# One buffer for the residual, deeper scratch, ScalarE in the preparation, and new orders for every engine

## The chip, the cores and the metric

The kernel runs on one core of one Trainium2 chip. A core has TensorE (PE), VectorE (DVE), ScalarE (ACT), GpSimd (POOL) and SyncE (SP), which here issues all DMAs. The metric is the device time of one launch in microseconds, from the inputs in memory to `out_y` in memory.

## What is computed

The reference is two transformer layers on x of shape (16, 256, 256), in float32. Each sublayer is added to its input and layer-normalised.

```python
x = L0_attn_x                                   # (16, 256, 256), heads of 16
x = _layernorm(x + _L0_attn_ref(x, ...))        # stage a
x = _layernorm(x + _L0_ffn_ref(x, ...))         # stage g, first half
x = _layernorm(x + _L1_attn_ref(x, ...))        # stages g (qkv), b, e
x = _layernorm(x + _L1_ffn_ref(x, ...))         # stage c
# _L0_attn: q, kv = x @ W.T; both through an fft over 16, l2-normalised per head;
#           kv summed over the sequence (cumsum); product; ifft; @ W_o.T
# _L0_ffn : 8 experts; gate = sigmoid(slope * (sum((w_n . (x - m_n)/|x - m_n|)**2) - center));
#           the best expert's low-rank update (rank 8) and bias, mixed with x by the gate
# _L1_attn: softmax attention, 16 heads of 16, on a qkv reshaped without a transpose
# _L1_ffn : ternary weights (groups of 64): W -> sign-like {-1,0,1} * mean|W|;
#           h = relu(x @ w1.T)**2; rmsnorm(h) @ w2.T, hidden 1024
```

The order of the batches is free, since each of the 16 is computed alone.

## The kernel before, in words

Everything of a batch is two sides of 128 partitions with 256 columns. A batch goes through stages whose names begin with a letter: `a` (first attention), `g` (gated feed-forward, and then q, k and v of the second attention), `b` (the maxima of the scores, the pass before the softmax), `e` (scores, exponentials, output), `c` (ternary feed-forward). `w` is the preparation of weights, which is done once, `p` the load of x.

Each engine runs a list of steps of its own. A step is a short Python function of the same name that waits for semaphores and issues a few instructions. `turns` (L605) walks three lists one after the other for each engine: FILL, written out as `step@batch`, up to turn 8; then ORDER, in which `step:+shift` means the batch that is that many turns behind (with the stage's lag in LAG, L97), repeated for turns 8 to 13; then DRAIN, written out again. Within an engine nothing passes anything else: a step that waits holds all that is behind it in its list. So the lists and the semaphores together set the time, and several batches are under way at once (in the middle, stage `c` works on the batch five behind the one in stage `a`).

The preparation starts with five loads on SP, all counted by one semaphore, `dft_in`: constants, the two DFT matrices and three weights. PE multiplies weights by the DFT matrices into pA and pC. DVE splits each product into a rounded high part (`fp32r`) and the difference (L1295, L1296), copies the inverse one (L1298), splits the qkv weights in the same way (`w_qkv_split`, L1332, L1333), and makes the ternary weights: `w_scale` casts 2,048 columns to bf16 (L1257) and reduces them, four `w_sign` steps compare and multiply them, PE turns them (`w_turn`) and ACT copies them out. Every one of these DVE instructions waits for the one before it (`prep`).

A batch's second residual lives in three places. `g_res2` and `g_norm2` write it into `x2`; `b_keep` on ACT copies `x2` into `xb[k]`, one of two; `e_res` adds the attention's output and writes `x3[k]`, one of two, from which stage `c` reads until `c_res`. `g_res2` of the next batch waits for the copy of this one.

For the second attention q and k are split into three bf16 parts (high, middle, low), written to scratch in memory (`g_out_0`, `g_out_1`, `g_out_2`) and read back in another layout (`g_in_0` with six DMAs, `g_in_1` with four, `g_in_2` with two). The scratch is two deep for q and k and one deep for v. `b_max_0`, PE's first score product of the max pass, waits for all twelve. PE then alternates between two banks, which DVE's maxima (`b_max_read`, L1545) free; the row maxima go back into qT by way of `b_rows`. `g_gate1` and `g_gate2` on DVE are the gate's small steps, with `g_exp` on ACT between them.

Of the kernel before, what the change touches and what calls it, by code (L numbers as in the profile page):

```python
# [107 lines left out]

# [7 lines left out]

# [1684 lines left out]
```

## Time and profile before

| | us |
|---|---|
| median of three runs (lowest, highest) | 824.48 (819.50, 828.29) |
| the profiled execution | 822.42 |
| its span, first to last instruction | 820.4 |

| engine | busy us | share |
|---|---|---|
| PE | 679.6 | 83% |
| DVE | 595.2 | 73% |
| ACT | 477.4 | 58% |
| POOL | 354.0 | 43% |

The mean granted clock of TensorE is 0.931 of full speed. The profile's page cuts the span into 40 slices of 20.5 us and gives each engine's busy tenths in each. Tables by stage give the same sums in microseconds for a chosen stretch. A timeline row is one instruction, or several alike that follow one another, with the idle time before it in square brackets and what ended it.

### The profile page before, as it was taken

The numbers are of one execution on the slowest core, as the hardware profiler recorded it, in microseconds if no ns is written. First come the engines' busy times: TensorE is split into PE (matmuls) and PEld (weight loads), VectorE is DVE, ScalarE is ACT, GpSimd is POOL, SyncE is SP. The second block draws the span as 40 slices with busy tenths as digits, with TensorE's granted clock in tenths as the row PEclk, the third lists the DMA queues.
The fourth block names the chain that finished last, engine by engine and source line by source line (L and its number), as shares of the span: only waits on it lengthen the run. The fifth ranks groups of instructions, "written<-read, shape, count | busy, mean of one in ns | idle before, by whom it ended". The sixth has DMA issues, their size and how long they took to land.

```text
span 820.4 us, 14805 instructions
## 1 busy us (share of the span) xinstructions
PE 679.6 (83%) x5100; PEld 530.1 (65%) x5100; DVE 595.2 (73%) x1429; ACT 477.4 (58%) x961; POOL 354.0 (43%) x537
## 2 busy tenths in 40 slices
PE   3545667788999999999999999899997998888773
PEld 3324545465777778787777777777776776656462
DVE  3977548687888797979797879688888877457120
ACT  0123232646767677777676767677657485755930
POOL 3214202112536464645454645352647253354554
PEclk9667688999999999999999999999999999999976
DMA  6100044716071617171617162506162525350000
GB/s 210 51 0 14 14 71 104 131 19 136 13 140 37 120 41 138 34 138 32 135 37 133 39 136 49 119 26 111 33 111 71 96 61 85 83 118 28 14 13 14
DMA packets 298170, 60.57 MB, mean 74 GB/s; under 512 B 237352, under 2 KB 293616, under 8 KB 298096
## 3 DMA queue, kind: packets, MB, share of 16 engines
q1 hardware_dynamic: 298096, 59.63, 36.0%
q8 instruction: 41, 0.67, 0.3%
q14 instruction: 33, 0.27, 0.1%
HBM read 38.38 MB, written 20.97 MB: 72 GB/s over the span
## 4 chain that ended last, share of the span: by engine, by line
PE 41%; DVE 20%; SPq 14%; DMA 9%; ACT 6%; issue 5%; POOL 5%; POOLq 0%; DVEq 0%; ACTq 0%
SPq L710 9%; PE pA L892 7%; DVE nmax L1545 6%; PE pB L908 5%; PE pA L807 4%; PE pO L960 4%; DMA kT<-qk_scratch 4%; DMA qk_scratch<-qk_part 3%; PE pC L1009 3%; PE pC L1031 3%; SPq L696 2%; PE pS L934 2%; PE pS L984 2%; PE pA L791 2%; DMA xa<-in_x 1%
## 5 line engine op out<-in xcount | busy, mean ns | idle before, releaser
L1545 DVE TENSOR_REDUCE nmax<-pB 128x2 f32<-128x512 f32 x256 | 167.5, 682 | 49.5 <-PE pB L908 48.7
L1160 ACT ACTIVATE pt<-pS 128x512 f32<-128x512 f32 x256 | 149.4, 605 | 84.6 <-PE pS L934 83.3
L908 PE MATMUL pB<-kT,qT 96*128 96x256 bf16 x512 | 93.5, 284 | 30.0 <-DMA kT<-qk_scratch 15.7
L1720 POOL TENSOR_TENSOR hsum<-hsum,hsq 128x512 f32<-128x512 f32 x48 | 63.0, 1312 | 86.3 <-ACT hsq L1200 86.3
L934 PE MATMUL pS<-qT,kT 98*128 98x256 bf16 x512 | 88.5, 277 | 6.8 <-ACT pt L1160 5.4
L1743 POOL TENSOR_TENSOR hid_lo<-hh,hid 128x512 fp32r<-128x512 f32 x64 | 86.1, 1345 | 2.9 <-ACT hh L1210 2.6
L908 PEld LDWEIGHTS pB<-kT,qT 96*128 96x128 bf16 x512 | 40.0, 100 | 60.7 <-DVE nmax L1545 32.7
L1009 PE MATMUL pC<-x3T,w1T 128*128 128x256 f32 x256 | 71.2, 311 | 4.3 <-ACT hr L1188 2.6
L960 PE MATMUL pO<-pt,v_ext 128*32 128x256 f32 x1024 | 71.0, 397 | 3.7 <-ACT pt L1160 3.6
L1009 PE MATMUL pC<-x3T_lo,w1T 128*128 128x256 f32 x256 | 65.4, 289 | 0.0
L934 PEld LDWEIGHTS pS<-qT,kT 98*128 98x128 bf16 x512 | 42.4, 98 | 34.7 <-ACT pt L1160 16.1
L1031 PE MATMUL pC<-w2T,hid 128*128 128x256 f32 x256 | 63.7, 290 | 0.8 <-DVE ms L1605 0.8
L892 PE MATMUL pA<-xgT,w_qkv 128*128 128x256 f32 x192 | 60.5, 315 | 2.8 <-ACT qkv L1123 1.9
L1031 PE MATMUL pC<-w2T,hid_lo 128*128 128x256 f32 x256 | 61.9, 283 | 0.0
L892 PE MATMUL pA<-xgT,w_qkv_lo 128*128 128x256 f32 x192 | 55.7, 290 | 0.0
L892 PE MATMUL pA<-xgT_lo,w_qkv 128*128 128x256 f32 x192 | 55.7, 290 | 0.0
L1009 PEld LDWEIGHTS pC<-x3T,w1T 128*128 128x128 f32 x256 | 50.5, 197 | 6.8 <-ACT hr L1188 3.9
L1665 POOL TENSOR_SCALAR vea<-mva 128x2 f32<-128x2 f32 x16 | 5.4, 337 | 112.6 <-DVE mva L1346 112.6
L1009 PEld LDWEIGHTS pC<-x3T_lo,w1T 128*128 128x128 f32 x256 | 50.8, 198 | 0.0
L1031 PEld LDWEIGHTS pC<-w2T,hid 128*128 128x128 f32 x256 | 49.1, 192 | 1.5 <-DVE ms L1605 1.0
L1123 ACT COPY qkv<-pA 128x512 f32<-128x512 f32 x48 | 29.9, 622 | 34.7 <-PE pA L892 34.6
L1031 PEld LDWEIGHTS pC<-w2T,hid_lo 128*128 128x128 f32 x256 | 49.2, 192 | 0.1
(175 smaller groups left out, 1750.2 us busy)
## 6 DMA issues: line engine op xcount, KB each, us to landing
qk_scratch<-qk_part SPq DMA_DIRECT2D x48, 256.0 KB, 5.1
...
xa<-in_x SPq DMA_DIRECT2D x16, 256.0 KB, 3.8
v_scratch<-qkv SPq DMA_DIRECT2D x16, 256.0 KB, 3.4
v_heads<-v_scratch SPq DMA_DIRECT2D x16, 256.0 KB, 3.1
out_y<-y SPq DMA_DIRECT2D x16, 256.0 KB, 3.0
...
```

The source lines that it names most:

```text
L710: sp.dma_start(dst[r:STACK:PARTS, :].rearrange("d (h n) -> d h n", h=HEADS), scratch[k, n].rearrange("(w h d n) -> w d h n", w=2, h=HEADS, ...
L807: ins = pe.matmul(dst, part, w, start=(first and n == 0), stop=(last and n == 2))
L892: ins = pe.matmul(pA[1][:, half * T:(half + 1) * T], w[:, c, cols], part[:, c, :], start=(c == 0 and q == 0), stop=(c == CH - 1 and q == 2))
L908: ins = pe.matmul(pB[h % 2][:, s * T:(s + 1) * T], qT[k][0:STACK, u * P:(u + 1) * P], kT[k][0:STACK, h * T:(h + 1) * T], start=True, stop= ...
L934: ins = pe.matmul(pS[h % 2][:, s * T:(s + 1) * T], kT[k][:, u * P:(u + 1) * P], qT[k][:, h * T:(h + 1) * T], start=True, stop=True)
L960: ins = pe.matmul(pO[32 * j:32 * (j + 1), (g % 2) * T:(g % 2 + 1) * T], v_ext[:, u, :], pt[:, g % 2, j, s, :], start=(s == 0), stop=(s == ...
L1009: ins = pe.matmul(pC[:, e * T:(e + 1) * T], w1T[:, c, hc * P:(hc + 1) * P], part[:, c * T:(c + 1) * T], start=(c == 0 and part is x3T), st ...
L1031: ins = pe.matmul(pC[:, s * D:(s + 1) * D], part[:, hc, s * P:(s + 1) * P], w2T[:, hc, :], start=(hc == 0 and part is hid), stop=(hc == HC ...
L1160: act.activation(pt[:, (h // 4) % 2, h % 4].rearrange("p s n -> p (s n)"), pS[h % 2][:], ACT.Exp, scale=HD ** -0.5).then_inc(S["probs"], 1)
L1545: dve.tensor_reduce(nmax[:, h * SIDES:(h + 1) * SIDES], pB[h % 2][:].rearrange("p (s k) -> p s k", s=SIDES), AX.X, ALU.max, negate=True).t ...
L1720: pool.tensor_tensor(hsum[:], hsum[:], hsq[:], ALU.add).then_inc(S["hsum_done"], 1)
L1743: pool.tensor_tensor(hid_lo[:, 2 * g:2 * g + 2].rearrange("p c n -> p (c n)"), hh[:, g % 2, :], hid[:, 2 * g:2 * g + 2].rearrange("p c n - ...
```

## The change

It has four parts. The residual stays in `xr[i % 5]` from `g_res2` to `c_res`; `x2`, `xb` and `x3` and the step `b_keep` go, and the qkv weights are loaded into `xr[3]`, `xr[4]` and `y`. The scratch for q, k and v is four deep. ACT makes the high parts of both splits, the copy of the inverse DFT product and the bf16 casts, PE's first products go to pB and wait only for the loads that they need, and further waits of the preparation move to the step that needs them. And the FILL, ORDER and DRAIN lists of all engines are new, DRAIN beginning at turn 13.

```diff
+RESID = 5
+SLOTS = 4
...
-FILL_TURNS, DRAIN_TURN = 8, 14
+FILL_TURNS, DRAIN_TURN = 8, 13
...
-        x2 = sb("x2", [P, SIDES, D])
+        xr = [sb(f"xr{k}", [P, SIDES, D]) for k in range(RESID)]
-        xb = [sb(f"xb{k}", [P, SIDES, D]) for k in range(2)]
-        x3 = [sb(f"x3{k}", [P, SIDES, D]) for k in range(2)]
-        w_qkv_in = (x3[0], x3[1], y)
+        w_qkv_in = (xr[3], xr[4], y)
...
+            sp.dma_start(dfts, const[:, CONST_COLS:]).then_inc(dft_in, 16)
+            sp.dma_start(raw[:, 0], wq.rearrange("(c p) n -> p c n", p=P)).then_inc(dft_in, 16)
+            sp.dma_start(raw[:, 1], wkv.rearrange("(c p) n -> p c n", p=P)).then_inc(wkv_in, 16)
+            sp.dma_start(cst[:], const[:, 0:CONST_COLS]).then_inc(cst_in, 16)
+            sp.dma_start(raw[:, 2], woT.rearrange("(c p) n -> p c n", p=P)).then_inc(wo_in, 16)
...
# g_out_0, and g_v_out in the same way
-                    if has(i, 2):
-                        sp.wait_ge(S["qk_in"], before(i, PER["qk_in"], back=2))
+                    if has(i, SLOTS):
+                        sp.wait_ge(S["qk_in"], before(i, PER["qk_in"], back=SLOTS))
...
# PE
-            pe.wait_ge(dft_in, 16 * 5)
             for w in range(2):
+                if w:
+                    pe.wait_ge(wkv_in, 16)
+                else:
+                    pe.wait_ge(dft_in, 16 * 2)
...
# ACT
+            for w in range(2):
+                act.wait_ge(dft_ready, w + 1)
+                for n in range(CH):
+                    src, hi, _ = spectra_parts(w, n)
+                    act.copy(hi, src).then_inc(spec_hi, 1)
+            def w_unspec_sb(i, k):
+                act.wait_ge(dft_ready, 3)
+                act.copy(w_unspec[:].rearrange("p c n -> p (c n)"), pC[:]).then_inc(unspec_ready, 1)
+            def w_qkv_hi(i, k, n):
+                act.wait_ge(w_in, 16 * 12)
+                for half in range(2):
+                    part, hi, _ = qkv_parts(n, half)
+                    act.copy(hi, part).then_inc(qkv_hi, 1)
+            def w_cast(i, k, w):
+                act.wait_ge(tern_in, 16 * (w + 1))
+                if w:
+                    act.wait_ge(tern_ready, 1)
+                else:
+                    act.wait_ge(dft_ready, 3)
+                act.copy(tern_b, tern_w).then_inc(tern_used, 1)
-            def b_keep(i, k):
...
# DVE
-                prep(dve.tensor_copy(tern_b, tern_w))
-                    prep(dve.tensor_copy(hi, src))
-            prep(dve.tensor_copy(w_unspec[:].rearrange("p c n -> p (c n)"), pC[:]))
-                    prep(dve.tensor_copy(hi, part))
...
-                if has(i):
-                    dve.wait_ge(S["xb_copied"], before(i, PER["xb_copied"]))
+                if has(i, RESID):
+                    dve.wait_ge(S["c_res_done"], before(i, PER["c_res_done"], back=RESID))
+                elif i >= 3:
+                    dve.wait_ge(qkv_w_ready, 1)
...
             def e_res(i, k):
+                r = xr[i % RESID][:].rearrange("p s n -> p (s n)")
                 dve.wait_ge(S["wo_ready"], nth(i, PER["wo_ready"], 1))
+                dve.tensor_tensor(r, r, pS[0][:], ALU.add).then_inc(S["wo_read"], 1)
```

Of the lists these parts matter below. The repeated ORDER of PE and DVE, cut to the stretch from the last qkv product to the maxima, with the shifts left out:

```diff
# PE, from g_qkv_2 to b_max_0
-g_qkv_2 e_outt_0 b_max_13 b_max_14 a_proj_0 e_outt_1 b_max_15 a_proj_1 c_ms e_ont a_cum b_maxt_t e_wo
-g_mixt c_y e_score_0 e_score_1 g_mix a_prt e_vt e_score_2 e_score_3 c_x3t a_attn e_score_4 c_hid_0
-e_out_0 e_score_5 e_score_6 c_hid_1 e_score_7 e_score_8 g_x1t e_out_1 g_gate b_max_0 e_score_9 b_max_1
+g_qkv_2 b_max_11 b_max_12 e_out_3 b_max_13 b_max_14 e_outt_0 b_max_15 e_outt_1 a_proj_1 c_ms b_maxt_t
+e_ont a_cum e_vt e_wo g_mixt c_y e_score_0 e_score_1 g_mix e_score_2 a_prt e_score_3 c_x3t e_score_4
+a_attn e_out_0 e_score_5 e_score_6 c_hid_0 e_score_7 e_score_8 c_hid_1 g_x1t e_out_1 e_score_9
+e_score_10 g_gate e_score_11 b_max_0 b_max_1 a_xt c_hid_2 b_max_2 e_score_12 g_x2t b_max_3 e_out_2
+b_max_4 e_score_13 b_max_5 g_qkv_0 e_score_14 b_max_6 c_hid_3 b_max_7 b_max_8 g_qkv_1 a_proj_0
# DVE
-b_max_read_8 a_spectra_1 b_max_read_9 b_max_read_10 g_gate2_0 b_max_read_11
+b_max_read_5 g_gate1_4 g_gate1_5 a_inverse g_gate2_0 b_max_read_6 b_max_read_7 g_gate2_1
# ACT
-g_qkv_sb_0 c_hsq_2 e_exp_13 g_exp
+c_relu_2 g_qkv_sb_0 e_exp_13 g_exp c_h_2
# SP
-g_v_out c_store p_load g_v_in g_out_0 b_rows g_out_1 g_out_2 g_in_0 g_in_1 g_in_2
+g_v_out g_v_in c_store g_out_0 b_rows g_out_1 g_in_0 g_out_2 g_in_1 g_in_2 p_load
```

And the first steps of FILL (preparation steps without their @0):

```diff
# DVE
-w_gate_prod w_qkv_split_0 w_qkv_split_1 a_xt_lo@0 w_qkv_split_2 w_scale_0 w_sign_0_0 a_sums@0 a_xt_lo@1
-w_sign_0_1 w_sign_0_2 a_inverse@0 a_spectra_0@0 a_spectra_1@0 w_sign_0_3 w_bias a_even@0 a_cross@0
-a_products_0@0 a_products_1@0 w_scale_1 w_sign_1_0 w_sign_1_1 a_res1@0 a_bn@0 a_mean@0 w_sign_1_2
-a_norm1@0 a_sums@1 w_sign_1_3 g_gate1_0@0
+w_gate_prod w_qkv_split_0 a_xt_lo@0 w_qkv_split_1 w_qkv_split_2 w_scale_0 w_sign_0_0 w_sign_0_1
+a_sums@0 w_sign_0_2 w_sign_0_3 w_bias a_xt_lo@1 a_inverse@0 a_spectra_0@0 a_spectra_1@0 w_scale_1
+w_sign_1_0 w_sign_1_1 a_even@0 a_cross@0 a_products_0@0 a_products_1@0 w_sign_1_2 w_sign_1_3 a_res1@0
+a_bn@0 a_mean@0 a_norm1@0 a_sums@1 a_xt_lo@2 g_gate1_0@0
# ACT
-a_xt_sb@0 a_proj_sb_0@0 a_proj_sb_1@0 a_squares@0 a_xt_sb@1
+w_qkv_hi_0 w_qkv_hi_1 w_qkv_hi_2 w_unspec_sb a_xt_sb@0 w_cast_0 a_proj_sb_0@0 a_proj_sb_1@0 a_xt_sb@1
+a_squares@0 w_cast_1 w_turn_sb_0
# PE
-w_gate a_xt@0 a_proj_0@0 a_proj_1@0 a_xt@1
-... g_x2t@0 a_xt@3 g_qkv_0@0 g_qkv_1@0 g_qkv_2@0 a_proj_0@3
+a_xt@0 a_proj_0@0 a_proj_1@0 a_xt@1 w_gate
+... g_x2t@0 g_qkv_0@0 a_xt@3 g_qkv_1@0 a_proj_0@3 g_qkv_2@0 a_proj_1@3
# SP
-p_load@0 w_load w_load_fc p_load@1 w_load_proj p_load@2
+w_load p_load@0 w_load_fc w_load_proj p_load@1 p_load@2
```

## Rows read from the trace of the kernel before

**Rows 1.** The profile's page: busy time of each engine, then PE's tenths by slice.

```profile
PE 679.6 (83%) x5100; PEld 530.1 (65%) x5100; DVE 595.2 (73%) x1429; ACT 477.4 (58%) x961; POOL 354.0 (43%) x537
...
PE   3545667788999999999999999899997998888773
```

**Rows 2.** Busy time by stretch: PE, PEld, DVE, ACT, POOL, clock, DMA share, GB/s.

```profile
0.00:61.60 61.60, 28.58 (x92) 20.20 (x92) 42.53 (x64) 10.18 (x26) 16.16 (x23) 0.75 0.28 87
310.00:515.00 205.00, 194.93 (x1592) 158.32 (x1592) 173.40 (x435) 146.31 (x291) 106.30 (x165) 1.00 0.44 86
515.00:725.00 210.00, 187.27 (x1503) 146.97 (x1501) 161.34 (x383) 137.84 (x272) 98.25 (x135) 0.96 0.41 82
```

**Rows 3.** Instruction groups, turns: count, busy us, mean ns, idle before, releaser.

```profile
L1545 DVE TENSOR_REDUCE nmax<-pB 128x2 f32<-128x512 f32 x256 | 167.5, 682 | 49.5 <-PE pB L908 48.7
...
L908 PE MATMUL pB<-kT,qT 96*128 96x256 bf16 x512 | 93.5, 284 | 30.0 <-DMA kT<-qk_scratch 15.7 <-DVE nmax L1545 13.5
...
L960 PE MATMUL pO<-pt,v_ext 128*32 128x256 f32 x1024 | 71.0, 397 | 3.7 <-ACT pt L1160 3.6
...
L1123 ACT COPY qkv<-pA 128x512 f32<-128x512 f32 x48 | 29.9, 622 | 34.7 <-PE pA L892 34.6
...
L1147 ACT COPY xb<-x 128x512 f32<-128x512 f32 x16 | 9.9, 621 | 2.7 <-DVE x L1584 2.7
...
L1476 DVE TENSOR_SCALAR gt<-gt 128x16 f32<-128x16 f32 x16 | 4.3, 268 | 4.2 <-ACT gt L1104 4.1
```

**Rows 4.** Timeline of DVE, 0 to 100 us: start, duration, line, operation, idle before.

```profile
12.77 0.42 DVE L1295 CAST w_spec<-pA 128x256 fp32r<-128x256 f32 x1 [4.03 <-PE pA L762]
...
33.72 1.28 DVE L1379 TENSOR_REDUCE ss<-spec 128x32 f32<-128x512 f32 x2
...
44.53 0.55 DVE L1385 RECIPROCAL rn<-root_t 128x64 f32<-128x64 f32 x1 [4.41 <-POOL root_t L1695]
...
61.62 0.69 DVE L1427 TENSOR_TENSOR x<-xa,pA 128x512 f32<-128x512 f32 x1
...
71.60 0.44 DVE L1449 TENSOR_TENSOR f<-pA,g_bias 128x272 f32<-128x272 f32 x1 [0.81 <-PE pA L854]
```

**Rows 5.** Instruction groups of the preparation.

```profile
L1279 DVE TENSOR_TENSOR pt<-pt,prep_in 128x2048 f32<-128x2048 f32 x2 | 4.6, 2276 | 0.0
...
L1257 DVE CAST prep_in<-pt 128x2048 bf16<-128x2048 f32 x2 | 2.5, 1228 | 0.3 <-DVE w_qkv_lo L1333 0.2
...
L1295 DVE CAST w_spec<-pA 128x256 fp32r<-128x256 f32 x4 | 1.7, 424 | 4.1 <-PE pA L762 4.0
...
L1332 DVE CAST w_qkv<-x 128x256 fp32r<-128x256 f32 x4 | 1.6, 395 | 0.2
...
L1298 DVE COPY w_unspec<-pC 128x512 f32<-128x512 f32 x1 | 0.7, 691 | 0.0
```

**Rows 6.** Timeline of ACT, 20 to 55 us.

```profile
21.82 0.58 ACT L1073 CAST xT<-pA 128x512 fp32r<-128x512 f32 x1 [19.82 <-PE pA L791]
...
30.53 1.06 ACT L1086 ACTIVATE spec<-raw_spec 128x1024 f32<-128x1024 f32 x1
```

**Rows 7.** Timeline of PE, the first product.

```profile
7.31 5.43 PE L762 MATMUL pA<-qkv,prep_in 128*128 128x256 f32 x16 [7.31 <-DMA prep_in<-in_woT]
```

**Rows 8.** Timeline of SP's issues, 380 to 433 us: g_in_0's first, g_in_2's last.

```profile
395.32 4.14 SPq L710 DMA_DIRECT2D qT<-qk_scratch  x3
...
406.02 0.61 SPq L710 DMA_DIRECT2D kT<-qk_scratch  x1
```

**Rows 9.** Timeline of PE, b_max_0 in the middle and at 531 us.

```profile
408.74 0.39 PE L908 MATMUL pB<-kT,qT 96*128 96x256 bf16 x2 [1.19 <-DMA kT<-qk_scratch]
...
531.48 0.39 PE L908 MATMUL pB<-kT,qT 96*128 96x256 bf16 x2 [2.33 <-DMA kT<-qk_scratch]
```

**Rows 10.** DMA issues: count, KB each, median us to landing.

```profile
qk_scratch<-qk_part SPq DMA_DIRECT2D x48, 256.0 KB, 5.1
```

**Rows 11.** Busy time by stretch, behind the wait at 531 us.

```profile
532.00:536.00 4.00, 4.00 (x25) 2.75 (x23) 3.70 (x7) 3.46 (x8) 3.50 (x3) 0.63 0.19 67
```

More of the change, by code:

```diff
@@ L98 @@
 ORDER = (
[25 rows of a table removed]
-    "g_mean a_res1 a_bn a_mean a_norm1 "
-    "c_rms:+3 e_pow:+3 c_pow:+3 a_pow1:+2 g_pow2:+2 c_norm:+3 a_root_0:+1 a_root_1:+1 c_lo_0:+2 "
-    "a_root_2:+1 a_root_3:+1 a_root_4:+1 c_add_1:+2 c_lo_1:+2 c_add_2:+2 c_lo_2:+2 c_add_3:+2 c_lo_3:+2 "
-    "c_hsum:+2 "
-    "g_v_out:+4 w_load_fc:+3 c_store:+4 w_load_proj:+3 p_load:+2 g_v_in:+4 g_out_0:+3 b_rows:+3 w_load:+2 "
-    "g_out_1:+3 g_out_2:+3 g_in_0:+3 g_in_1:+3 g_in_2:+3 "
[31 rows of a table added]
 ).split()
-FILL_TURNS, DRAIN_TURN = 8, 14
+FILL_TURNS, DRAIN_TURN = 8, 13
 FILL = (
[105 rows of a table removed]
[102 rows of a table added]
 ).split()
 DRAIN = (
[119 rows of a table removed]
[148 rows of a table added]
     "g_mean@15 g_norm2@15 g_x2t_lo@15 b_max_read_0@14 b_max_read_1@14 b_max_read_2@14 b_max_read_3@14 "
     "b_max_read_4@14 b_max_read_5@14 b_max_read_6@14 b_max_read_7@14 b_max_read_8@14 b_max_read_9@14 "
[34 rows of a table removed]
[33 rows of a table added]
 ).split()
@@ L436, in mega_kernel @@
                 wfc, wproj, const, out):
-    scratch = nc.dram_tensor("qk_scratch", [2, 3, 2 * T * D], BF16).ap()
-    v_scratch = nc.dram_tensor("v_scratch", [T * D], F32).ap()
+    scratch = nc.dram_tensor("qk_scratch", [SLOTS, 3, 2 * T * D], BF16).ap()
+    v_scratch = nc.dram_tensor("v_scratch", [SLOTS, T * D], F32).ap()
     with ExitStack() as ctx:
@@ L633, in mega_kernel, with spectra_parts, qkv_parts @@
         vals = qkv[:, 2 * ROWS:].rearrange("p n h -> p (n h)")
+        def spectra_parts(w, k):
+            src = pB[w][:, k * D:(k + 1) * D].rearrange("p (c n) -> p c n", c=2)
+            hi, lo = (v[:, k].rearrange("p (c q n) -> p c q n", c=2, q=2)[:, :, w] for v in (w_spec, w_spec_lo))
+            return src, hi, lo
+        def qkv_parts(n, half):
+            src = w_qkv_in[n][:].rearrange("p c (j s d) -> p s c d j", s=2, d=HD)[:, half]
+            cols = slice((2 * n + half) * P, (2 * n + half + 1) * P)
+            hi, lo = (v[:, :, cols].rearrange("p c (d j) -> p c d j", d=HD) for v in (w_qkv, w_qkv_lo))
+            return src, hi, lo
         block = ctx.enter_context(nc.Block())
@@ L716, in g_v_out @@
                 apart(sp)
-                if has(i):
-                    sp.wait_ge(S["v_in"], before(i, PER["v_in"]))
+                if has(i, SLOTS):
+                    sp.wait_ge(S["v_in"], before(i, PER["v_in"], back=SLOTS))
                 apart(sp)
-                sp.dma_start(v_scratch.rearrange("(h p n) -> p h n", p=P, n=2 * HD),
+                sp.dma_start(v_scratch[i % SLOTS].rearrange("(h p n) -> p h n", p=P, n=2 * HD),
                              vals.rearrange("p (h n) -> p h n", n=2 * HD)).then_inc(S["v_out"], 16)
@@ L1141, in e_vt_sb @@
                          pO[:].rearrange("p (s h d) -> p s h d", s=SIDES, d=HD)).then_inc(S["v_ready"], 1)
-            def b_keep(i, k):
-                act.wait_ge(S["x2_done"], nth(i, PER["x2_done"], 2))
-                if has(i, 2):
-                    act.wait_ge(S["wo_read"], before(i, PER["wo_read"], back=2))
-                act.copy(xb[k][:].rearrange("p s n -> p (s n)"), x2[:].rearrange("p s n -> p (s n)")
-                         ).then_inc(S["xb_copied"], 1)
             def e_exp(i, k, h):
@@ L1218, in c_hi @@
                                ).then_inc(S["hi_done"], 1)
-            steps = dict(b_keep=b_keep, g_first=g_first, g_mid=g_mid, e_vt_sb=e_vt_sb, a_xt_sb=a_xt_sb, a_squares=a_squares, a_prt_sb=a_prt_sb, g_x1t_sb=g_x1t_sb,
+            steps = dict(w_unspec_sb=w_unspec_sb, g_first=g_first, g_mid=g_mid, e_vt_sb=e_vt_sb, a_xt_sb=a_xt_sb, a_squares=a_squares, a_prt_sb=a_prt_sb, g_x1t_sb=g_x1t_sb,
                          g_exp=g_exp, g_mixt_sb=g_mixt_sb, g_x2t_sb=g_x2t_sb, e_ont_sb=e_ont_sb,
@@ L1228, in _ @@
                 steps[f"w_turn_sb_{n}"] = lambda i, k, n=n: w_turn_sb(i, k, n)
+                steps[f"w_cast_{n}"] = lambda i, k, n=n: w_cast(i, k, n)
+            for n in range(3):
+                steps[f"w_qkv_hi_{n}"] = lambda i, k, n=n: w_qkv_hi(i, k, n)
             for n in range(HEADS):
@@ L1325, in w_qkv_split @@
             def w_qkv_split(i, k, n):
-                dve.wait_ge(w_in, 16 * 12)
                 for half in range(2):
-                    part = w_qkv_in[n][:].rearrange("p c (j s d) -> p s c d j", s=2, d=HD)[:, half]
-                    cols = slice((2 * n + half) * P, (2 * n + half + 1) * P)
-                    hi, lo = (v[:, :, cols].rearrange("p c (d j) -> p c d j", d=HD) for v in (w_qkv, w_qkv_lo))
-                    prep(dve.tensor_copy(hi, part))
+                    part, hi, lo = qkv_parts(n, half)
+                    dve.wait_ge(qkv_hi, 2 * n + half + 1)
                     prep(dve.tensor_tensor(lo, part, hi.bitcast(F32), ALU.subtract))
```

72 lines of the change are left out of this document (31 added, 41 removed), and 595 rows, old and new, of tables (DRAIN, FILL, ORDER).

## The prediction

> **What bounds the kernel now.** I read the page's totals and slices first. TensorE (PE) is busy 83% of the span and VectorE (DVE) 73%, but the slices show three regimes: PE near full in the middle, thin before slice 7 and thin in the last slices [rows 1]. Tables by stage give them sizes. From 310 to 515 us PE is busy 194.93 of 205 us at full clock; from 515 to 725 it is 187.27 of 210 at clock 0.96; up to 61.6 us, where the first batch reaches its first residual, PE has 28.58 us of work at clock 0.75, while DVE has 42.53 [rows 2]. From 310 to 515 us 1,592 matmuls fill 194.93 us, 0.12 us each [rows 2], which is what 256 columns take one behind the other, so PE really is occupied. A turn, one batch's worth of all stages, is 5100/16 = 319 matmuls [rows 1], 41.0 us at that rate. PE's idle time in it is mostly one wait at b_max_0, the first score product of the max pass, for the last piece of kT to land. These waits are the larger part of the 30.0 us that PE stands before that product in the whole run: 15.7 us on the DMA, the rest on DVE [rows 3]. So three things can move the time: the DVE chain of the preparation, the wait at b_max_0, and new stalls from the new orders.
>
> **The preparation.** Before the first residual the chain runs on DVE nearly without a break: the first weight copy at 12.77 us, a_sums at 33.72, the reciprocal at 44.53, the residual at 61.62 [rows 4]. The change gives ScalarE (ACT) four copies of 0.424 us, one of 0.69, six of 0.40 and two of 1.228 [rows 5]: 1.70 + 0.69 + 2.39 + 2.46 = 7.2 us off DVE. ACT has nothing to do until 21.82 us and little after [rows 6]. The price there: a copy of 512 columns is 0.58 us and 1,024 columns 1.06 [rows 6], so 2,048 columns extrapolate to 2.0 us; w_cast_0 then ends at about 19.5 us on ACT, and DVE, which still has two weight differences to make, reaches w_scale_0 at about 20. It is covered by half a microsecond; without cover it costs that overhang, under 1 us. w_cast_1 has DVE wait for nothing: ACT can make it while DVE waits for POOL's root.
>
> The Trainium skill (ScalarE: Activation LUTs, Rules for kernel authors) says to keep plain adds, multiplies and relus on VectorE, which would speak against moving the casts; its figures give 186 + 0.833 x 2048 = 1.89 us as an estimate for the 2,048-column cast, near the 2.0 above. The trace agrees on the large cast (1.228 us on DVE), not on a PSUM source of 512 columns (0.69 on DVE, 0.58 on ACT). By that rule, with both casts on the path, the sum would be about 1.5 us worse.
>
> PE's first products start at 7.31 us, when all five first loads have landed [rows 7]; the new wait is for two of the five and a later one for the third, worth 0 to 2 us; I take 1, since the two are now the first issues but the five fly together. Against this the new list puts work ahead of the residual: w_sign_1_2 and w_sign_1_3, 2.28 us each [rows 5], which used to come behind it; and w_sign_0_1 now stands ahead of a_sums, where 4.41 us of idle time for POOL's root was [rows 4] and about 3.7 stays. Sum at the residual: -7.2 -1 -0.7 -0.5 (small gaps) +4.6 = -4.8. But DVE then owes nothing more to the preparation, and between there and the first gate 4.6 us of it used to run, some of it in POOL's shadow; I count 1.2 of it. **Term 1: -6 us**, bounds -3 (casts uncovered, no earlier start) and -9.
>
> New waits of the preparation: p_load@1 now stands behind w_load_proj on the SP queue, which waits for w_cast_0. x of batch 1 lands some 10 us later, at about 26, and ACT's a_xt_sb@1 stands ahead of a_squares@0. The squares would end at about 28, when DVE reaches a_sums at about 28: no cost, up to 2 us if the loads are slow; inside the bound. w_gate@0 waits for gate weights behind the same a_xt; its user, the bias, is needed only at the first gate.
>
> **The residual buffer.** b_keep goes: 16 copies of 0.621 us on ACT [rows 3]. ACT is busy 146 of 205 us even in the middle [rows 2], so its 0.6 us per turn are worth 0; if ACT were the bound they would be worth 10. g_res2 of batch i now waits for c_res of batch i-5, which comes before it in DVE's own queue: nothing new is late. The qkv_w_ready wait for batches 3 and 4 is long past. Deeper scratch in memory takes away waits on reads that are two turns (one for v) old: 0.
>
> **The wait at b_max_0.** In PE's new order the steps between g_qkv_2 and the next b_max_0 gain e_out_3, two b_max and three e_score and lose a_proj_0. e_out_3 is 16 of the 1,024 matmuls that take 71.0 us together [rows 3], 1.1 us; the other five are two matmuls each at 0.12 us, 1.2 us; a_proj_0 is six of double width, 1.5 us. So PE comes 0.8 us later, with work done in between. On SP g_in_0, six issues, moves ahead of g_out_2. An issue takes 0.61 us, in a full queue 4.14 for three [rows 8], so the six take 3.7 to 8.3 us. Before, the twelve issues began at 395.32, behind g_out_2, and ended at 406.6, and PE could start at 408.74, 2.1 us later [rows 8, 9]. The new train can begin some 2.7 us sooner, at about 392.6; g_out_2 is then issued at 396.3 to 400.9, lands 5.1 us later [rows 10], two issues and a landing follow, and the last pieces are there at 404.7 to 409.3: 4 us earlier to 0.6 later. The waits are 1.19 us in the middle, 2.33 at 531 [rows 9]. I take half of the 15.7: **term 2: -7 us**, bounds 0 and -15.7. What is late next is DVE's maximum; PE already stands for it for about as long.
>
> **The clock.** Behind the long waits the granted clock falls: 0.63 from 532 to 536, after the wait of 2.33 us [rows 9, 11], that is between the level of 1.2 GHz and that of 2.4. Such a stretch loses 4 x 0.37 = 1.5 us, and the mean of 0.96 from 515 to 725 [rows 2] makes 0.04 x 210 = 8.4 us. Shorter waits spare some: **term 3: -3 us**, bounds 0 and -8.
>
> **Sum:** 822.4 (the profiled execution; its span is 820.4) - 6 - 7 - 3 = 806.4. That execution lies 2.1 us below the median of the three runs, 824.48; I say 807.
>
> **Rivals.**
> A, the forecast: 798 to 816, chance 0.55.
> B, the new lists also mend the end. From 515 to 725 PE stands 22.7 us, from 310 to 515 only 10.1 [rows 2]; if the end ran as the middle, 12.6 us would go, of which about half is already in terms 2 and 3. Time 807 - 6 to - 14, about 794. For it: nearly the same work is there; against: that a new list removes stalls is not visible in it. Chance 0.20.
> C, the gain is absorbed. After the preparation PE of batch 0's qkv is interleaved with batch 3's projection (2.5 us at half clock between g_qkv_1 and g_qkv_2), so the first b_max_0 gains less than term 1, and the wait at b_max_0 only moves to DVE's maximum. Then 822.4 - 3 to - 5, about 819. Chance 0.14.
> D, slower: DVE's g_gate2_0 moves from behind b_max_read_10 to ahead of b_max_read_6. It waits for ACT's g_exp, which stands behind g_qkv_sb_0 and e_exp_13, and g_qkv_0 itself is on PE only after b_max_5. From b_max_5: 12 matmuls (1.5 us), the copy 0.622 [rows 3], an activation of the same size and the gate's small exp, together some 3.0 us, while DVE has some 1.9 us to do (a maximum of 0.682 [rows 3], two gate steps, the reciprocal of 0.55 [rows 4]). It stands 1.1 us, b_max_read_6 behind it, and PE's b_max_7 needs that. If ACT is late by one more instruction it is 1.7. Over 13 turns 14 to 22 us come on: with term 1 alone, 831 to 838, 834. It outweighs term 1 from 0.5 us per turn, and is a measurable loss from 1.1. Against: in the trace before DVE waits only 4.1 us in all for that exp [rows 3]. Chance 0.11.
>
> **Numbers.** 1% of 824.5 is 8.2 us, about what a measurement can tell: faster is below 816, slower above 833. A and B are faster but for a sliver, C is the same, D is mostly slower: faster 0.78, same 0.14, slower 0.08. The range holding 8 in 10 runs from 788 (B with term 2 at its bound) to 822 (C whole, D left out).
>
> **What would show it.** Term 1: the first residual at about 56 us and the first gate product's read 6 us before 71.6; if it is later than 60 the step failed. Term 2: PE idle before the max product on the DMA at or below 8 us, turns of 40 us or less in the middle. Term 3: no 4 us stretch below 0.8 after 200 us. B: end stretches of the same batches as short as middle turns. D: DVE idle on ACT's gate exp above 10 us in all, and PE's idle on DVE's maximum grown. A turn above 41 us in the middle would make the prediction wrong whatever the preparation gives.

## The result, and the profile after

The changed kernel takes 790.66 us (median of 4 runs, 789.01 to 794.39) where the kernel before, timed beside it, takes 822.99 (4 runs, 819.5 to 828.29): a ratio of 0.9608, 95% interval 0.9544 to 0.9673. It is faster, as forecast, and inside the range of 788 to 822, but the gain of 3.9% is about twice the 2% that was said. A few executions of any of these kernels come out longer at a lower granted clock; the ratios leave them out.

The page after, in the form of [rows 1]: busy time of each engine, then the tenths of PE and of its granted clock by slice.

```profile
PE 667.5 (85%) x5100; PEld 525.6 (67%) x5100; DVE 588.1 (75%) x1416; ACT 474.9 (60%) x958; POOL 347.2 (44%) x537
...
PE   5466658799998999999989999989999998888763
...
PEclk9668578999999999999999999999999999999965
```

The same 5,100 matmuls, and 12.1 us less busy time for them: a busy time that falls with an unchanged count can be clock, or matmuls that no longer wait inside. To see where, I cut both traces at the same events: the first maximum that DVE reads of batches 0, 4, 10 and 15. Busy time of PE by these stretches, with clock, DMA share and GB/s; before:

```profile
0.00:61.60 61.60, 28.58 (x92) 0.75 0.28 87
61.60:130.00 68.40, 43.20 (x175) 0.72 0.26 50
130.00:286.60 156.60, 138.54 (x1071) 0.99 0.44 82
286.60:531.90 245.30, 231.67 (x1890) 1.00 0.44 87
531.90:737.90 206.00, 182.93 (x1472) 0.96 0.40 79
737.90:820.40 82.50, 54.71 (x409) 0.85 0.05 18
```

and after:

```profile
0.00:57.10 57.10, 28.67 (x94) 0.77 0.31 94
57.10:121.50 64.40, 42.32 (x172) 0.71 0.25 49
121.50:271.50 150.00, 136.96 (x1078) 0.99 0.46 89
271.50:516.00 244.50, 229.52 (x1891) 1.00 0.44 87
516.00:705.50 189.50, 174.30 (x1472) 0.99 0.43 84
705.50:788.20 82.70, 55.70 (x405) 0.82 0.06 18
```

The 32.2 us between the two spans are 8.5 up to batch 0's first maximum, 6.6 in the second part of the ramp (batches 0 to 4), 0.8 in the middle (4 to 10), 16.5 at the end (10 to 15), and -0.2 in the last stretch. The end, which the forecast's sum priced at nothing of its own, gave half in these two profiles; in the second part of the ramp, for which no term of it stood either, PE's idle time fell from 18.1 to 13.0 us.

The steps of the prediction, in the rows of after. DVE's chain of the preparation, as in [rows 4] (start, duration):

```profile
28.55 1.28 DVE L1438 TENSOR_REDUCE ss<-spec 128x32 f32<-128x512 f32 x2
...
39.07 0.55 DVE L1444 RECIPROCAL rn<-root_t 128x64 f32<-128x64 f32 x1 [3.44 <-POOL root_t L1751]
...
57.08 0.69 DVE L1486 TENSOR_TENSOR x<-xa,pA 128x512 f32<-128x512 f32 x1 [1.20 <-PE pA L890]
...
64.35 0.43 DVE L1508 TENSOR_TENSOR f<-pA,g_bias 128x272 f32<-128x272 f32 x1
```

and the groups of the turns, as in [rows 3]:

```profile
L1606 DVE TENSOR_REDUCE nmax<-pB 128x2 f32<-128x512 f32 x256 | 165.7, 679 | 34.8 <-PE pB L960 34.2
L960 PE MATMUL pB<-kT,qT 96*128 96x256 bf16 x512 | 90.5, 278 | 25.8 <-DVE nmax L1606 16.9 <-DMA kT<-qk_scratch 8.2
L1012 PE MATMUL pO<-pt,v_ext 128*32 128x256 f32 x1024 | 68.5, 385 | 4.6 <-ACT pt L1229 4.5
...
L1535 DVE TENSOR_SCALAR gt<-gt 128x16 f32<-128x16 f32 x16 | 4.6, 286 | 0.6 <-ACT gt L1180 0.6
```

The first residual is 4.5 us earlier and the gate 7.3. PE's first product starts at 5.26 us where it had started at 7.31:

```profile
5.26 5.06 PE L807 MATMUL pB<-qkv,prep_in 128*128 128x256 f32 x11 [5.26 <-DMA prep_in<-in_wq]
```

PE's idle time before the max product fell by 4.2 us in all, but the wait on the DMA fell from 15.7 to 8.2 while that on DVE's maximum rose from 13.5 to 16.9. DVE waits 0.6 us for the gate's exp, so rival D never began. By stretch (total us, times, longest), PE's waits in the middle before; those of after stand under reads:

```profile
PE pB L908 <- DMA kT<-qk_scratch: 6.9, 6, 2.3
PE pB L908 <- DVE nmax L1545: 6.1, 15, 1.3
```

and at the end (batches 10 to 15), before and then after; `on` is the attention's normalised output:

```profile
PE pB L908 <- DMA kT<-qk_scratch: 6.8, 4, 2.5
PE pO L791 <- DVE on L1573: 3.0, 4, 1.6
```

```profile
PE pB L960 <- DMA kT<-qk_scratch: 3.1, 3, 1.6
PE pO L837 <- DVE on L1634: 1.1, 2, 0.6
```

### The profile page after: what moved, and what is told of

The parts are those of the page before. It is cut to its first block, busy times and chain, and to the rows that moved or that the text cites. A ratio compares the mean times of both kernels' runs of the same rounds, so it can differ in the third digit from the quotient of the medians.

```text
span 788.2 us, 14764 instructions
## 1 busy us (share of the span) xinstructions
PE 667.5 (85%) x5100; PEld 525.6 (67%) x5100; DVE 588.1 (75%) x1416; ACT 474.9 (60%) x958; POOL 347.2 (44%) x537
## 4 chain that ended last, share of the span: by engine, by line
PE 35%; DVE 29%; SPq 13%; DMA 7%; POOL 7%; issue 6%; ACT 4%; POOLq 0%; DVEq 0%; ACTq 0%
SPq L752 10%; DVE nmax L1606 9%; PE pB L960 4%; DMA kT<-qk_scratch 4%; PE pA L944 4%; PE pC L1083 3%; PE pO L1012 3%; DMA qk_scratch<-qk_part 3%; PE pA L837 3%; PE pA L855 3%; PE pC L1061 3%; PE pA L890 3%; PE pS L986 2%; DVE spec L1448 2%; PE pS L1036 2%
## 5 line engine op out<-in xcount | busy, mean ns | idle before, releaser
L1606 DVE TENSOR_REDUCE nmax<-pB 128x2 f32<-128x512 f32 x256 | 165.7, 679 | 34.8 <-PE pB L960 34.2
L1229 ACT ACTIVATE pt<-pS 128x512 f32<-128x512 f32 x256 | 147.7, 605 | 61.1 <-PE pS L986 60.7
L960 PE MATMUL pB<-kT,qT 96*128 96x256 bf16 x512 | 90.5, 278 | 25.8 <-DVE nmax L1606 16.9
L1776 POOL TENSOR_TENSOR hsum<-hsum,hsq 128x512 f32<-128x512 f32 x48 | 64.7, 1348 | 59.5 <-ACT hsq L1269 59.3
L986 PE MATMUL pS<-qT,kT 98*128 98x256 bf16 x512 | 86.5, 276 | 4.5 <-ACT pt L1229 3.4
L1799 POOL TENSOR_TENSOR hid_lo<-hh,hid 128x512 fp32r<-128x512 f32 x64 | 84.3, 1316 | 5.3 <-ACT hh L1279 5.0
L1012 PE MATMUL pO<-pt,v_ext 128*32 128x256 f32 x1024 | 68.5, 385 | 4.6 <-ACT pt L1229 4.5
L1721 POOL TENSOR_SCALAR vea<-mva 128x2 f32<-128x2 f32 x16 | 3.6, 223 | 147.8 <-DVE mva L1405 147.7
L944 PE MATMUL pA<-xgT,w_qkv 128*128 128x256 f32 x192 | 58.5, 305 | 2.0 <-DVE xgT_lo L1591 1.7
L1721 POOL TENSOR_SCALAR veb<-mvb 128x2 f32<-128x2 f32 x16 | 3.7, 230 | 105.7 <-DVE mvb L1405 105.7
```

What stands on the lines that cost most here:

```text
L944: ins = pe.matmul(pA[1][:, half * T:(half + 1) * T], w[:, c, cols], part[:, c, :], start=(c == 0 and q == 0), stop=(c == CH - 1 and q == 2))
L960: ins = pe.matmul(pB[h % 2][:, s * T:(s + 1) * T], qT[k][0:STACK, u * P:(u + 1) * P], kT[k][0:STACK, h * T:(h + 1) * T], start=True, stop= ...
L986: ins = pe.matmul(pS[h % 2][:, s * T:(s + 1) * T], kT[k][:, u * P:(u + 1) * P], qT[k][:, h * T:(h + 1) * T], start=True, stop=True)
L1012: ins = pe.matmul(pO[32 * j:32 * (j + 1), (g % 2) * T:(g % 2 + 1) * T], v_ext[:, u, :], pt[:, g % 2, j, s, :], start=(s == 0), stop=(s == ...
L1229: act.activation(pt[:, (h // 4) % 2, h % 4].rearrange("p s n -> p (s n)"), pS[h % 2][:], ACT.Exp, scale=HD ** -0.5).then_inc(S["probs"], 1)
L1606: dve.tensor_reduce(nmax[:, h * SIDES:(h + 1) * SIDES], pB[h % 2][:].rearrange("p (s k) -> p s k", s=SIDES), AX.X, ALU.max, negate=True).t ...
```

## The experiments

A ratio is to runs of the kernel before on the same chip. The stretches are those of one profiled execution of each, in us, cut as above, so they carry the scatter of a single execution, that of the clock above all; the ratio is of several:

| kernel | to batch 0 | 0 to 4 | 4 to 10 | 10 to 15 | last | ratio (95% interval) |
|---|---|---|---|---|---|---|
| before | 130.0 | 156.6 | 245.3 | 206.0 | 82.5 | 1 |
| after | 121.5 | 150.0 | 244.5 | 189.5 | 82.7 | 0.9608 (0.9544-0.9673) |
| struct | 122.6 | 156.9 | 243.5 | 201.3 | 82.6 | 0.9915 (0.9871-0.9959) |
| lists_oldcode | 133.4 | 154.8 | 247.6 | 187.7 | 81.6 | 0.9821 (0.9788-0.9855) |
| h_end_old | 122.7 | 150.2 | 256.1 | 203.9 | 82.6 | 0.9929 (0.9891-0.9966) |
| h_end_new | 122.5 | 157.0 | 249.2 | 189.4 | 84.7 | 0.9778 (0.9750-0.9806) |
| before_sp | 131.0 | 165.5 | 242.4 | 210.1 | 84.7 | 1.0167 (1.0113-1.0221) |
| before_fill | 131.3 | 156.6 | 245.1 | 199.5 | 87.8 | 1.0003 (0.9967-1.0039) |
| end_old_sp | 121.7 | 149.2 | 252.6 | 200.0 | 82.5 | 0.9854 (0.9784-0.9924) |
| reads | 122.4 | 150.2 | 240.2 | 188.8 | 84.3 | 0.9582 (0.9520-0.9644) |
| slots2 | 122.5 | 148.9 | 243.5 | 187.0 | 83.2 | 0.9560 (0.9514-0.9606) |
| prep_dve | 127.1 | 149.2 | 243.1 | 188.9 | 84.7 | 0.9665 (0.9608-0.9721) |
| tail | 119.4 | 150.3 | 243.8 | 188.8 | 78.9 | 0.9535 (0.9493-0.9576) |
| better | 122.3 | 149.0 | 239.1 | 188.2 | 78.8 | 0.9486 (0.9442-0.9530) |
| before_warm | 131.1 | 158.5 | 245.0 | 200.2 | 86.4 | 1.0008 (0.9980-1.0036) |
| better_warm | 123.7 | 149.0 | 238.1 | 187.0 | 74.9 | 0.9441 (0.9402-0.9480) |
| better_sp | 123.0 | 148.7 | 237.7 | 188.5 | 82.1 | 0.9471 (0.9424-0.9517) |

**struct: the code without the lists.**

```diff
 after.py, all five lists as in before.py, but on ACT
+w_qkv_hi_0@0 w_qkv_hi_1@0 w_qkv_hi_2@0 w_unspec_sb@0 a_xt_sb@0 w_cast_0@0 ...
+a_proj_sb_1@1 w_cast_1@0 w_turn_sb_0@0 ...
-b_keep@0 ... b_keep@15
```

> The changed code (residual in one of five buffers, scratch four deep, ScalarE's parts of the preparation) with the order lists of before; only ScalarE's six new steps are put in where they are due. Theory L (the new lists mended the end, the code itself only shortens the preparation): first residual some 4 us earlier and nothing else, 815 to 819 us; the stretch from batch 10's first maximum to batch 15's stays at 206 us. Theory S (the copy of the residual and the one-deep scratch were what held the old order up): 795 to 802 us, the same stretch near 190 us.

Measured: 818.6 us (median of 9; the ratio makes it 815), inside theory L's range. The runs fall in two groups, 808.8 to 812.5 and 818.6 to 819.4 us (one more at 823.0), and the profile is one of the first group (808.83), so its stretches flatter this kernel. It is shorter by 7.4 us up to batch 0, by 1.8 in the middle and by 4.7 at the end. At the end PE's idle time is nearly as before (22.0 us, before 23.1); what differs is the clock, 0.98 instead of 0.96. The code alone is worth about 0.9% of the 3.9 (0.4 to 1.3).

**h_end_old and h_end_new: the end's order.**

```diff
 after.py, every engine's list:
 h_end_old:  the new one up to turn 13, then the rest in the order of before
 h_end_new:  that of before up to turn 14, then the rest in the new order
```

> The changed kernel whose lists are the new ones up to turn 13, and from there on every engine takes its remaining steps in the order of before. Theory L: 790.7 + 16.5 (what the stretch of batches 10 to 15 lost between the two profiles) = 807 us, between 802 and 812. Theory S: 791 to 795, since the code is the changed one.

> The changed code with the lists of before up to turn 14, and from there on every engine takes its remaining steps in the new order. Theory L: the time of the kernel 'struct' less what the order of the end is worth: 817 - 12 to 16 = 801 to 805 (a turn of the end is over by then). Theory S: within 3 us of the kernel 'struct'.

Measured: 814.9 us for h_end_old, 3 us above theory L's range, since the seam, the place where the two sets of lists meet, itself cost 11.6 us ahead of batch 10 (see end_old_sp); its end is 203.9 us. 802.52 us for h_end_new, as theory L had it, with an end of 189.4. Three kernels with the new end (with the changed code, with the old ramp, with the old code) have it at 187.7 to 189.5 us; three with the old one at 201.3 to 206.0. The order of the end is the cause of the short end, whatever code and ramp stand before it.

The ratios give the whole gain in three steps: the code 0.9% (struct), the order of the end another 1.4% (h_end_new against struct), and the order before the end another 1.7% (after against h_end_new). So the order before the end is worth about as much as that of the end. Most of it is the ramp of batches 0 to 4: 156.9 and 157.0 us in struct and h_end_new with the old order, 150.0 and 150.2 in after and h_end_old with the new one. A part of the rest is the seam of h_end_new (249.2 us in the middle).

**lists_oldcode: the lists without the code.**

```diff
 before.py with the lists of after.py, on ACT
+b_keep@i ahead of c_x3t_sb@i-2 (behind g_x2t_sb@i for i < 2)
-w_qkv_hi_n, w_unspec_sb, w_cast_n
 on SP: g_v_out@10 behind g_v_in@9
```

> The code of before (one residual and its copy by ScalarE, scratch two deep and one deep, VectorE prepares alone) with the new lists; ScalarE's copy is put in where its buffer comes free, and one load of the values is moved ahead of the next store, as the one-deep scratch needs. Theory L: 790.7 + 6 to 8.5 for the preparation + up to 2 for the copies = 797 to 801 us. Theory S: 812 us or more, because the new order then waits for the copy or the scratch.

Measured: 806.7 us, between the two theories. The end is as short as after's; what is missing against after is 11.9 us before batch 0, where the old preparation sits under lists made for another, 4.8 in the ramp and 3.1 in the middle. In these two DVE waits for the copy of the residual. The group, and one such wait with ACT's copy ahead of it:

```profile
L1610 DVE SCALAR_TENSOR_TENSOR x<-x,two_less,pA 128x256 f32<-128x256 f32 x32 | 13.9, 477 | 11.4 <-ACT xb L1245 11.0 <-PE pA L969 0.4
```

```profile
235.22 0.87 DVE L1610 SCALAR_TENSOR_TENSOR x<-x,two_less,pA 128x256 f32<-128x256 f32 x2 [3.33 <-ACT xb L1245]
```

```profile
234.47 0.61 ACT L1245 COPY xb<-x 128x512 f32<-128x512 f32 x1
```

The copy takes 0.61 us of ACT, which is nothing; that DVE's next residual has to come behind it has DVE stand 11.0 us in 8 waits (where I put the copy in is a choice, though it can't stand ahead of e_res of two batches ago). With the old lists DVE hardly waits there; the same group of the kernel before:

```profile
L1512 DVE SCALAR_TENSOR_TENSOR x<-x,two_less,pA 128x256 f32<-128x256 f32 x32 | 13.8, 473 | 0.2
```

So the buffers are worth nothing there, and under the new lists at most the 7.9 us that ramp and middle are longer by. That these are the copy's is argued from the waits: this kernel also has the old preparation and the shallow scratch, one deep for v, and no run puts the copy alone into after.

**slots2: scratch two deep.**

```diff
-SLOTS = 4
+SLOTS = 2
```

> The changed kernel with its scratch in memory two deep instead of four, for queries, keys and values (the residual still in five buffers). If the deeper scratch carries a part of the gain: SyncE's stores wait for the loads of two batches ago, 793 to 797 us. If it is worth nothing, as the prediction priced it: 789 to 793 us. The rest of the new order's need (the kernel of the old code with the new lists waited 11.0 us in 8 places for the residual's copy) is then the residual's.

Measured: 786.2 us, even below the expected 789 to 793, with an interval that overlaps after's. The deeper scratch for q and k shows no worth. A scratch of one for v, as in the kernel before, wasn't tried with the new code.

**prep_dve: ScalarE's share given back.**

```diff
-                    dve.wait_ge(spec_hi, CH * (w + 1))
+                    dve.wait_ge(dft_ready, w + 1)
+                    prep(dve.tensor_copy(hi, src))
...
-                dve.wait_ge(tern_used, w + 1)
+                dve.wait_ge(tern_in, 16 * (w + 1))
...
+                prep(dve.tensor_copy(tern_b, tern_w))
+                dve.sem_inc(tern_used, 1)
```

(and likewise for w_unspec and w_qkv; ACT's six steps go).

> The changed kernel, except that VectorE makes the high parts, the casts and the copy of the preparation again, with ScalarE's six steps gone; the loads are still waited for one by one and the lists are the same. If ScalarE's share is the gain of the preparation (the first step of the prediction, 6 us): first residual at 61 to 63 us instead of 57.1, 790.7 + 4 to 7 = 795 to 798. If most of it is the earlier first product (5.3 instead of 7.3 us): 791 to 794.

Measured: 794.52 us, on the edge between the two and with an interval that overlaps after's, but the trace decides: the first residual is at 62.64 us instead of 57.08, 5.6 us later. To batch 0's first maximum it is 5.6 us more as well, and no other stretch grew by more than 2.

```profile
62.64 0.69 DVE L1465 TENSOR_TENSOR x<-xa,pA 128x512 f32<-128x512 f32 x1 [1.20 <-PE pA L890]
```

**before_sp: the second step alone.**

```diff
 before.py, SP's list, every batch
-g_out_1 g_out_2 g_in_0 g_in_1 g_in_2
+g_out_1 g_in_0 g_out_2 g_in_1 g_in_2
```

> The kernel before, code and lists, except that on SyncE g_in_0 (six transfers, some 6 us of issuing) stands ahead of g_out_2 for every batch. Theory I (the waits 'on DMA' at b_max_0 are SyncE's issuing behind g_low, 10 us of it, and this takes six of the ten away): the waits of 6.9 us in the middle and 6.8 us at the end go, VectorE's maximum takes back some 3.8 of the middle as in the changed kernel, and two or three of the end's clock dips of 1.7 us go with their waits: 822 - 3 - 7 - 4 = 808 us. Theory B (g_in_0 then waits for part 0 to land and for the scores of two batches ago, and holds g_out_2 behind it): 820 to 826 us.

Measured: 835.02 us, slower than either theory said. PE's waits in batches 0 to 4 (total, times, longest):

```profile
PE pB L1005 <- DMA kT<-qk_scratch: 6.3, 2, 4.3
```

where before has 2.1 us. In the middle the move does what theory I says, in small: kT's wait goes from 6.9 to 3.5 us and the stretch from 245.3 to 242.4. In the ramp and at the end the stretches grow by 8.9 and 4.1 us. There SP reaches g_out_2 only behind the six issues and doesn't wait for its data (the step g_low of DVE), so the issues held it:

```profile
194.47 4.81 SPq L807 DMA_DIRECT2D qT<-qk_scratch  x3
199.33 1.91 SPq L807 DMA_DIRECT2D kT<-qk_scratch  x3
201.36 0.52 SPq L793 DMA_DIRECT2D qk_scratch<-qk_part  x1
```

Of the ramp's 8.9 us PE's idle time is only 3.4 (18.1 to 21.5); its clock fell too, from 0.99 to 0.95. The best place of g_in_0 seems to differ by batch, and the new lists don't have it in one place.

**end_old_sp: one engine's list of the end alone.**

```diff
 after.py, SP's list from turn 13 on as before
-... g_in_2@9 p_load@13 g_v_out@9 g_v_out@10 g_out_0@10 g_v_in@9 c_store@6 b_rows@9 ...
+... g_in_2@9 c_store@6 g_v_out@9 p_load@13 g_v_in@9 g_v_out@10 g_out_0@10 b_rows@9 ...
```

> The changed kernel, except that SyncE alone takes its steps from turn 13 on in the order of before (TensorE, ScalarE, VectorE and GpSimd keep the new one). If SyncE's order is what mended the end: 790.7 + 5 to 10 = 796 to 801 us, with TensorE's waits for kT back at b_max_0 of batches 13 to 15. If it is the order of the computing engines: 789 to 793.

Measured: 807.67 us, worse than expected. SP's issues, and PE behind them:

```profile
478.36 0.36 SPq L859 DMA_DIRECT2D out_y<-y  x1
478.91 0.37 SPq L835 DMA_DIRECT2D v_scratch<-qkv  x1
479.47 1.52 SPq L795 DMA_DIRECT2D xa<-in_x  x1
```

```profile
475.20 0.60 PE L1033 MATMUL pB<-kT,qT 96*128 96x256 bf16 x4
483.33 1.12 PE L910 MATMUL pA<-cst,xa 128*128 128x128 f32 x4 [7.53 <-DMA xa<-in_x]
```

The load of x stands behind the store of batch 6, for which SP sits until 478.36 us; with after's list the same load is issued at 470.34. PE stands 7.5 us for it. The same seam is in h_end_old, where PE's waits for x in the middle make 7.5 us too. The end after it is 200.0 us: from 460 us to its end PE waits 9.3 us for kT, where after has 5.4, and 5.2 for the row maxima, where after has none. In the kernel before the same SP list goes with the others' at no such price, so the lists are fitted to each other: SP's, taken from the other set, costs 2.5% (0.9854 against 0.9608), more than the whole order of the end gives. No run exchanges TensorE's, VectorE's, ScalarE's or GpSimd's list of the end alone, so which of them mends the end is open.

**before_fill and before_warm: the clock.** A dip is a stretch of some 3.4 us in which the granted clock is at 1.2 GHz; a filler is a matmul that nobody reads, which keeps PE busy.

```diff
                 if h == 0:
-                    pe.wait_ge(S["qk_in"], nth(i, PER["qk_in"], 192))
                     if has(i):
                         pe.wait_ge(S["maxt_sb"], before(i, PER["maxt_sb"]))
+                    for _ in range({10: 6, 11: 3, 12: 6, 14: 6}.get(i, 0)):
+                        pe.matmul(pB[0][:, 0:T], w_qkv[:, 0, 0:P], w_qkv[:, 0, 0:T], start=True, stop=True)
+                    pe.wait_ge(S["qk_in"], nth(i, PER["qk_in"], 192))
```

> The kernel before, except that TensorE, ahead of its wait for the transfers at b_max_0 of batches 10, 11, 12 and 14, runs 6, 3, 6 and 6 matmuls of 0.28 us into the bank that b_max_0 is about to overwrite; nothing reads them. The wait itself (2.3, 0.8, 2.2 and 2.5 us) stays. Theory C (the granted clock falls to half for some 3.4 us because TensorE had just stood idle, 1.7 us lost each time): the dips at 532, 576 and 704 us go, 822 - 5 = 817 us, and the end's mean clock rises from 0.96 to 0.98. Theory N (the dips come by themselves, whatever TensorE did before): as many dips as before, 822 to 823 us.

> The kernel 'before_fill' with fillers in batch 15's last stretch as well: TensorE runs 6 matmuls nobody reads ahead of c_x3t, 8 ahead of c_hid_0, 3 ahead of each other c_hid and 20 ahead of c_ms, before it waits there. The last stretch of the kernel before runs c_y at 1.2 GHz. If a dip avoided is time won: the last stretch falls from 82.5 to 76 to 79 us and the whole to 811 to 816 us. If not (the clock falls elsewhere instead, or the fillers take what they give): 819 to 823 us.

Measured: 822.25 and 822.45 us, no change. Six fillers took 0.96 us at 530.6, not the 1.7 I had reckoned, and the wait behind them was still 1.07. The end of before_fill and the last stretch:

```profile
533.00:732.50 199.50, 177.54 (x1486) 1.00 0.42 82
732.50:820.30 87.80, 61.13 (x409) 0.77 0.04 15
```

The five dips of the end are gone, down to one that begins as it ends, and the end is 6.5 us shorter; but the last stretch is 5.3 us longer, at clock 0.77 instead of 0.85. Its growth is clock, since PE's idle time there is 26.7 us where before has 27.8. With fillers there too (before_warm) its clock is 0.86 and it is still 86.4 us, with 62.3 us of PE busy instead of 54.7, fillers included. The three dips at filled waits (533, 577 and 704 us in before) are gone in both kernels, as theory C says. But so are the two at 635 and 680 us, whose waits of 1.7 and 1.6 us for DVE weren't filled and still last 1.6 us each in before_fill, so a part of it is scatter or follows from something else. The mechanism is likely, then, and not shown free of rivals, and its price for the whole kernel fails: the medians don't move. Why the clock falls more often in the last stretch is open; other kernels without fillers have such additional dips there too (reads, h_end_new).

**reads: DVE's maxima ahead of the gate.**

```diff
-    "g_gate1_3 b_max_read_5:+1 g_gate1_4 g_gate1_5 a_inverse g_gate2_0 b_max_read_6:+1 b_max_read_7:+1 "
-    "g_gate2_1 a_spectra_0 b_max_read_8:+1 w_bias:+1 g_gate2_2 g_gate2_3 b_max_read_9:+1 b_max_read_10:+1 "
+    "g_gate1_3 b_max_read_5:+1 g_gate1_4 b_max_read_6:+1 g_gate1_5 a_inverse b_max_read_7:+1 g_gate2_0 "
+    "g_gate2_1 a_spectra_0 b_max_read_8:+1 w_bias:+1 g_gate2_2 b_max_read_9:+1 g_gate2_3 b_max_read_10:+1 "
```

> The changed kernel, except that in the turns of the middle (batches 5 to 9) VectorE reads maximum 6 ahead of g_gate1_5 and a_inverse, maximum 7 ahead of g_gate2_0 and maximum 9 ahead of g_gate2_3. If the 0.93 and 0.67 us that TensorE waits in each turn for VectorE's maximum are a loss of their own: 5 x 1.6 = 8 us less, 782 to 785. If another wait stands behind them (the gate or the spectra come late and hold TensorE's g_mixt or a_cum): 788 to 791.

Measured: 787.51 us, between the two. PE's waits in the middle, after and then reads:

```profile
PE pB L960 <- DVE nmax L1606: 9.5, 17, 1.3
PE pB L960 <- DMA kT<-qk_scratch: 3.1, 2, 2.3
```

```profile
PE pB L960 <- DVE nmax L1606: 6.4, 10, 1.3
```

The middle is 4.3 us shorter in the profile: a third of the wait for DVE's maximum (3.1 us) went with this order, and the wait for kT fell by 2.1, to 1.0. The ratio's interval overlaps after's widely, so for the whole kernel the gain isn't shown by this run alone.

**tail, better, better_warm, better_sp: faster versions.**

```diff
 tail: for batch 15 c_add_1..3, c_hsum and c_norm leave POOL's list; on DVE
+            def d_add(i, g):
+                dve.wait_ge(S["hsq_done"], nth(i, PER["hsq_done"], g + 1))
+                dve.tensor_tensor(hsum[:], hsum[:], hsq[:], ALU.add).then_inc(S["hsum_done"], 1)
 better: reads and tail, with b_max_read_10 ahead of g_gate2_3 too
 better_warm: better, with before_warm's fillers in batch 15's steps
 better_sp: better, g_in_0 ahead of g_out_2 on SP for batches 9, 10, 11
```

> The changed kernel, except that for batch 15, with nothing behind it, VectorE instead of GpSimd sums the squares (three sums of 512 columns and one of 256) and normalises the output. TensorE stands idle 5.6 us there for GpSimd's chain of sums and parts: 2 us less; the normalising takes 2.4 us on GpSimd and some 0.9 on VectorE: 1.5 us less; 790.7 - 3.5 = 787 us. If the clock or the last store sets the end of the tail: no less than 789.

> The kernel 'reads' (787.5 us) with maximum 10 read ahead of g_gate2_3 as well, and the kernel 'tail' in it. If both gains are their own: 787.5 - 3.5 - up to 3 = 781 to 784 us. If the middle's next wait takes the place: 784 to 786.

> The kernel 'better' (779.3 us, its last stretch 78.8) with the same fillers in batch 15's last stretch. If a dip avoided is time won: c_y's 32 matmuls of 512 columns a pair run at 2.4 instead of 1.2 GHz, some 4 us less, and the whole 774 to 776 us. If not: 779 to 782 us.

> The kernel 'better' with g_in_0 ahead of g_out_2 on SyncE for batches 9, 10 and 11 too, as it is for most others. If TensorE's 2.3 us at b_max_0 of batch 10 are SyncE's issuing of ten microseconds behind g_low: 1.5 to 3 us less, 776 to 778 us. If g_in_0 itself has to wait there (for the scores of two batches ago) and holds g_out_2 and the rows behind it, as it did in the ramps of 'before_sp': 780 to 784 us.

Measured: tail 784.0 us with 3.8 us off the last stretch (PE's idle time there 23.8 us, after's 27.0), better 779.34, better_sp 777.88, which can't be told from better. The interval of tail still overlaps after's, that of better lies just below it. better_warm has the lowest median here, 775.93 us, 5.6% below before and clearly below after; its interval overlaps better's. Its last stretch:

```profile
697.80:772.70 74.90, 55.65 (x449) 0.96 0.06 20
```

In the profiles the clock (0.96, better's 0.86) goes with 3.9 us less in the stretch; better_sp, whose end of the lists is better's, has 0.81 and 82.1 us. The medians of better and better_warm are too near to show it for the whole.

## Why the prediction was right, and where it was wrong

**Term 1 (preparation, -6, bounds -3 to -9): right.** The residual came at 57.1 us (forecast 56, failed if over 60), the gate 7.3 us earlier. Giving ScalarE's share back moves the residual by 5.6 us: the mechanism is shown. The first product came 2.0 us earlier, where 1 was taken. To batch 0's first maximum it was 8.5 us.

**Term 2 (wait at b_max_0, -7): half right.** The wait on the DMA fell by 7.5 us over the run, to 8.2, where the threshold asked for 8. But in the middle the part that fell (6.9 to 3.1 us) came back as waiting for DVE's maximum (6.1 to 9.5), as rival C had it; the mean turn was 244.5 / 6 = 40.8 us (before 40.9) where 40 or less was asked, and the stretch gained 0.8. "What is late next is DVE's maximum" stood in the text, and should have been priced at the whole gain there. (The 41.0 us that the text gives a turn is 319 matmuls at 205/1,592 us, idle time included; at 0.12 us each they take 39.) In before_sp the moved issues alone gain 2.9 us in the middle and lose 13 in the ramp and at the end.

**Term 3 (clock, -3): the size was off.** Between batch 0's first maximum and batch 15's, before has six dips of 3.4 us at half clock, each worth 1.7 us of full clock, some 10 in all, five of them in the end; after has one, at 516 us, where the forecast's sign asked for none. Going by the two profiles that is some 7 us of the end's 16.5. What it is worth to the whole is less sure: struct's profile has two dips at the end with the same lists and nearly the same idle time as before, and the fillers took the dips away without moving the median.

**The residual's buffers (priced 0): too low under the new lists.** The price was read from ACT's 0.62 us. What the copy does there is to force an order on DVE: 11.0 us of waits in lists_oldcode, worth at most 7.9 us of time. The scratch (0) was right as far as it was tried.

**The step that failed: the stalls that the new lists remove, at the end above all, put at nothing in the sum.** Terms 2 and 3 together gave 10 us to all that comes behind batch 0's first maximum; it was 23.7 us. For the end the sum holds nothing of its own; it was rival B with a chance of 0.20 and a time of 794, against the 0.55 of A. It happened: the stretch of batches 10 to 15 fell by 16.5 us, PE's idle time in it from 23.1 to 15.2 (7.9 us) and the clock from 0.96 to 0.99. Waits on kT 6.8 to 3.1 us, on DVE's `on` 3.0 to 1.1. The text took it that "a new list removes stalls is not visible in it". But the room was: 22.7 us idle against 10.1 in the middle [rows 2], and five dips behind the waits. B's time was near (its own sum gives 793 to 801, the text 794); the chance was too low. Both its price and its chance could have been in the sum, at half. The forecast's range held the result only because its lower edge, 788, had been drawn for B.

The ramp of batches 0 to 4 is the other part, and there no rival had a price for it: its stretch fell by 6.6 us, PE's idle time in it by 5.1, spread over many waits of under 2 us. struct, h_end_new and h_end_old show that the new order does it, as above. Which steps of it do is open.
